# Two loads issued ahead of the last group's stores, and one sum moved from GpSimd to VectorE, in an AdaLN transformer layer

## The reference, cut to what matters

```python
x = data                                            # 2048 tokens x 1024
h = layernorm(x) * (1 + ca) + sa
x = x + ga * (h @ (weight * mask_by_32x32_blocks).T + bias)
h = layernorm(x) * (1 + cb) + sb                    # ca, sa, ... from silu(c) @ wmod
g = silu((h @ gate_w.T) * gate_s)                   # 2752 rows of gate_w, int32
u = (h @ up_w.T) * up_s
x = x + gb * (((g * u) @ down_w.T) * down_s)
```

## Time and profile before

| what | us |
|---|---|
| median of 3 runs | 1135.83 |
| the profiled execution | 1133.88 |
| its span | 1132.1 |
| TensorE busy | 1091.0 (96%) |
| VectorE busy | 787.1 (70%) |
| GpSimd busy | 412.1 (36%) |
| mean granted TensorE clock | 0.986 of full speed |

### The profile page before, as it was taken

How to read it: one execution, slowest core, us unless ns; L and a number is a source line. 1 busy time by engine, 2 the same in 40 slices (tenths; PEclk the granted TensorE clock), 3 DMA queues, 4 the chain that set the end, 5 groups by cost and what they waited for, 6 DMA issues and landing times. The chain is left out here.

```text
span 1132.1 us, 13073 instructions
## 1 busy us (share of the span) xinstructions
PE 1091.0 (96%) x4629; PEld 514.0 (45%) x4629; DVE 787.1 (70%) x966; ACT 423.3 (37%) x776; POOL 412.1 (36%) x365
## 2 busy tenths in 40 slices
PE   5996999999999999999999999999997999999998
PEld 3553554554444444434444444444443444444444
DVE  4789967767678898888897988879544343334434
ACT  0331236656555444445465555555432000000000
POOL 1223327546656363515675675755301000000000
PEclk9998989999999999999999999999998999999999
DMA  9993212426353565446676656665297666565430
GB/s 346 404 380 77 75 38 74 112 56 203 121 197 100 160 180 174 116 117 182 177 215 186 201 170 197 184 200 178 76 354 280 253 244 233 227 239 222 183 144 37
DMA packets 130000, 206.93 MB, mean 183 GB/s; under 512 B 20624, under 2 KB 99216, under 8 KB 127504
## 3 DMA queue, kind: packets, MB, share of 16 engines
q1 hardware_dynamic: 124640, 184.08, 49.4%
q0 software_dynamic: 5296, 22.02, 5.4%
HBM read 137.39 MB, written 68.68 MB: 182 GB/s over the span
## 5 line engine op out<-in xcount | busy, mean ns | idle before, releaser
L1295 PE MATMUL pA<-work 128*128 128x512 f16 x1680 | 378.6, 380 | 5.4 <-ACT work L1037 4.4
L1295 PEld LDWEIGHTS pA<-work 128*128 128x128 f16 x1680 | 164.1, 98 | 206.8 <-ACT work L1037 7.5
L1158 PE MATMUL pA<-work 128*128 128x512 f32 x512 | 227.2, 599 | 0.7 <-issue 0.7
L1295 PE MATMUL pB<-work 128*128 128x512 f16 x752 | 176.0, 379 | 1.8 <-DVE work L1726 1.8
L1748 DVE SCALAR_TENSOR_TENSOR work<-work 128x512 f16<-128x512 f16 x144 | 141.1, 1002 | 18.5 <-ACT work L1055 18.3
L1158 PEld LDWEIGHTS pA<-work 128*128 128x128 f32 x512 | 96.4, 193 | 113.4 <-issue 112.5
L1362 PE MATMUL pA<-work 128*128 128x512 f16 x600 | 136.1, 382 | 6.0 <-DMA work<-down_left_scratch 6.0
L912 ACT ACTIVATE work<-pB,small 128x128 f32<-128x128 f32 x256 | 92.7, 480 | 90.4 <-PE pB L1147 77.0
L1037 ACT ACTIVATE work<-pA 128x512 f32<-128x512 f32 x126 | 74.7, 593 | 114.6 <-PE pA L1295 108.6
L1295 PEld LDWEIGHTS pB<-work 128*128 128x128 f16 x752 | 73.4, 98 | 90.8 <-DVE work L1726 2.8
L1362 PE MATMUL pB<-work 128*128 128x512 f16 x480 | 107.5, 379 | 0.0
(11 more groups left out here) (170 smaller groups left out, 1159.4 us busy)
## 6 DMA issues: line engine op xcount, KB each, us to landing
work<-h_scratch SPq DMA_DIRECT2D x8, 4480.0 KB, 13.6
h_scratch<-work SPq DMA_DIRECT2D x60, 512.0 KB, 3.0
work<-in_L_wmod SPq DMA_DIRECT2D x10, 2048.0 KB, 18.0
work<-in_L_ffn_gate_w SPq DMA_DIRECT2D x84, 128.0 KB, 3.2
work<-in_L_ffn_up_w SPq DMA_DIRECT2D x84, 128.0 KB, 2.9
work<-down_scratch SPq DMA_DIRECT2D x7, 1280.0 KB, 15.6
work<-in_L_ffn_down_w SPq DMA_DIRECT2D x68, 128.0 KB, 2.8
work<-in_L_attn_data SPq DMA_DIRECT2D x16, 512.0 KB, 4.2
```

Source lines behind the costliest of these rows:

```text
L1158: last = pe.matmul(pA[:, 2 * par(t) + h, :], hT1[par(t)][:, c, :], wT[:, c, h * H:(h + 1) * H], start=(c == 0), stop=(c == KT - 1))
L1295: last = pe.matmul(ps, w[:, m, c], bc[b][:, mv_, s, c], start=begin, stop=(i == n - 1 and c == KT // 2 - 1 and s == 1), skip_group_check=True)
```

## The change

Two loads move in SP's queue: in pass NG - 1 wl and then WT1 are issued ahead of group 40's stores, and the wait for tail_ready in front of them goes (the stores of the tail one pass earlier have waited for the same count). For an odd chunk, S4 is no longer GpSimd's third operation: VectorE makes it, right after up[1] and ahead of the low part of S1, with a semaphore s4_ready of its own; s_ready now counts two for each odd group.

```diff
@@ SP, pass g
+                if g == NG - 1:
+                    sp.dma_start(wl..., wl_d...).then_inc(wl_loaded, 16)
+                    load_wd(WT1)
                 loads = [...]
                 ... the stores of group g - 1 ...
                 if g == NG - 1:
-                    sp.wait_ge(tail_ready, 4)
-                    load_wd(WT1)
-                    sp.dma_start(wl..., wl_d...).then_inc(wl_loaded, 16)
                     sp.wait_ge(p3_done, NG)
                     for m in (WT3, WT4, W22):
                         load_wd(m)
@@ GpSimd, odd_sums
-                pool.wait_ge(s_ready, n + 2)
-                pool.tensor_tensor(gate[1], up[0], keep[b][0], ALU.subtract).then_inc(s_ready, 1)
@@ ScalarE, hi_of
-                if m in (S1, S2, S4):
-                    act.wait_ge(s_ready, 3 * groups_before(g, "odd") + (S1, S2, S4).index(m) + 1)
+                if m in (S1, S2):
+                    act.wait_ge(s_ready, 2 * groups_before(g, "odd") + (S1, S2).index(m) + 1)
+                elif m == S4:
+                    act.wait_ge(s4_ready, groups_before(g, "odd") + 1)
@@ VectorE, wait_read
-                    dve.wait_ge(s_ready, 3 * groups_before(g - 1, "odd") + (3, 1)[half])
+                    dve.wait_ge((s4_ready, s_ready)[half], (1, 2)[half] * groups_before(g - 1, "odd") + 1)
@@ VectorE, pass g, behind hi_plus(up[1], ...)
                 if len(outs) > 2:
+                    dve.wait_ge(s_ready, 2 * groups_before(g - 1, "odd") + 2)
+                    dve.tensor_tensor(gate[1], up[0], keep[GROUPS[g - 1][1]][0], ALU.subtract).then_inc(s4_ready, 1)
+                if len(outs) > 2:
                     lo_of(g - 1, outs[2])
```

More of the change, by code:

```diff
@@ L349, in adaln_kernel @@
         s_ready = sem("s_ready")
+        s4_ready = sem("s4_ready")
         h2_hi = sem("h2_hi")
@@ L670, in _ @@
                         store_tail(sp, TAIL_BEFORE[g], half)
+                if g == NG - 1:
+                    sp.dma_start(wl.rearrange("p c k d -> p (c k d)"), wl_d.rearrange("p c k d -> p (c k d)")).then_inc(wl_loaded, 16)
+                    load_wd(WT1)
                 loads = [u for u in range(EARLY + 2, NUNIT) if g < NG and group_of[u - 2] == g]
@@ L697, in _ @@
                 if g == NG - 1:
-                    sp.wait_ge(tail_ready, 4)
-                    load_wd(WT1)
-                    sp.dma_start(wl.rearrange("p c k d -> p (c k d)"), wl_d.rearrange("p c k d -> p (c k d)")).then_inc(wl_loaded, 16)
                     sp.wait_ge(p3_done, NG)
@@ L838, in odd_sums @@
             def odd_sums(g):
-                b, n, before = GROUPS[g][1], 3 * groups_before(g, "odd"), partner(g)
+                b, n, before = GROUPS[g][1], 2 * groups_before(g, "odd"), partner(g)
                 pool.wait_ge(h2_lo, outs_until(before, S3))
```

## The result

Over twelve runs of each on the same chips, the changed kernel takes 1125.16 us (1122.59 to 1132.15) and the kernel before 1135.3 us (1132.66 to 1137.79): a ratio of 0.9916, 95% interval 0.9902 to 0.9930, or 9.5 us less (7.9 to 11.1; the two medians lie 10.1 apart). The forecast was 4.5 us less, 1131.3 (1127.3 to 1133.8).

What follows compares the result with a forecast made beforehand. The prediction took TensorE's waits as the bound. Removed 8.3 us (6.00 + 1.87 + 0.42), added stall 2.6 and clock 1.7, second stage -0.5: net -4.5, from 1135.83 to 1131.3 us, range 1127.3 to 1133.8.

Steps and rivals of the forecast that it cites:

- The loads, issued earlier: Down stage's start: wl and WT1 land near 855, removing a 6.00 us wait and 1.87 us of clock.
- the 0.42 us: Second stage's last product: its 0.42 us wait for VectorE would go, since up[1] is made sooner.
- What is late next: Pair 1's start: load_h2(1)'s small part lands at 892.4, TensorE is ready at 889.8, so it idles 2.6 us.
- The sum moved: Second stage: S4 on VectorE gives -0.5 us, bounds -1.5 and +1.6, besides the 0.42 us wait removed.
- the four places: Second stage, where TensorE's p7 needs the snapshot following gate[1]: each was to lose 0.25 us, 1.0 in all.
- kind (a): Odd groups whose low parts overlap L846: VectorE gains 0 to 0.1 us, up[1] comes sooner, two low parts take about 1.9.
- D: Rival: SP's queue for pair 1 gets no shorter, stall 7.6 us there; +0.7 us, 1136.5; chance 0.09.
- E: Rival: VectorE's subtraction lands on the path in all odd groups, 12 us; +8, 1143.8; chance 0.06.
- The 2.23 us stall: Second stage, TensorE behind VectorE's gate_b in an even group: claimed to stay at 2.23 us.
- the new stall and its clock: Pair 1's start: TensorE stalls 2.6 us, then loses 1.7 us to a lowered clock.
- B: Rival: the new stall at pair 1 costs no clock; -6.2 us, 1129.6; chance 0.23.
- C: Rival: pair 1's data comes sooner, stall 0.8 us or less; -8.0 us, 1127.8; chance 0.17.

Runs made afterwards that it cites:

- loads_only: Kernel before with only the two loads issued early, S4 still on GpSimd; 1128.05 us, ratio 0.9947.
- waits_loads: Kernel before with the two early loads and two redundant VectorE waits per odd group, last sum still on GpSimd; 1125.3 us, ratio 0.9913.
- gate_b_held: Changed kernel with VectorE's product of up[0] at gate_b made to wait for GpSimd's first sum of chunk 9; 1132.9 us, one run.
- small_first: Changed kernel with each pair's small load issued ahead of its big one; 1126.18 us, ratio 0.9914.
- after_again: Changed kernel, nothing altered, run and profiled a second time; 1125.51 us in one run.
- waits_after: Kernel before with two redundant VectorE waits only in the odd groups' passes behind group 13; 1137.68 us, one run.

## Why the prediction was off

**Right.** *The loads, issued earlier*: both waits and the 1.87 us of clock are gone, all 7.9 us; the 0.42 us, which the forecast credited to the sum, went with the sum, since loads_only keeps 0.41. wl and WT1 land at 848.0 and 851.9, 3 us sooner than said, because they begin 1.4 us sooner and move in the working time too: the window 841 to 850 now carries 394 GB/s where the earlier trace rows had 340. *What is late next*: the place, the transfer and the order were right; the issue of the small part was forecast 20.0 us after the down stage's start and came at 20.45, and TensorE was ready at 33.1 where 32.8 was said (0.17 us of this is the way of counting, 0.13 a gap between two products). *The sum moved*, taken proper: forecast -0.42 - 0.5 = -0.9 us, measured 507.42 - 508.35 = -0.9 against waits_loads. But its pieces differ, and that they add up is luck. The 1.54 us stall went and a 0.62 for VectorE came in its place at 408.27; the four places that were to lose 0.25 each, 1.0 in all, lost 0.16 at two (0.33 to 0.49) and nothing at two. GpSimd's L846 is gone and kind (a)'s low parts take 1.71 and 1.79 us for two, as said (1.9). Rivals D and E are refuted: the queue did get shorter, and the 20 subtractions (0.68 us each) cost nothing on the path. WT3 is issued 2.2 us after the down stage's start, WT1 was 1.7 after it.

**The step that failed:** "The 2.23 us stall comes from a chain (gate_b) in an even group and stays." It shrank by 1.23 us, and with it went the 1.7 us of clock behind it: 2.9 of the 6.0 us by which the traces differ from the forecast. The chain is as described, but it is fed by a collision 9 us earlier that 0.36 us in VectorE's stream decide. I asked which instructions the change touches, and not which neighbours were within a fraction of a microsecond of another order. The trace before had the sign: a product of 1.62 us begun 0.08 us behind a sum of GpSimd, where its like at 504.71 takes 0.75.

**The terms that were mis-sized:** the new stall and its clock, 2.6 + 1.7 = 4.3 us, measured 0.87 + 0 (0.87 to 1.85 in seven profiles of kernels without padding or a held product). The stall took 15.4 us for the landing; in the profiles with the early loads it is 13.4 to 15.7 and once 17.1, since the small load lands anywhere in that scatter, and 15.4 was one draw from its upper half. The eight pairs of the kernel before, which the forecast could have asked for, landed in 13.6 to 15.7 us, median 14.6 (after: 13.4 to 16.0, median 14.5). The median would have been the better choice, and gives a stall of 1.8. The clock followed from the stall: of the ten profiles in the table the eight with up to 1.85 us lost none, and those with 3.98 and 4.53 us lost 1.57 and 1.39. At 2.6 us itself nothing was run; at 2.2 us the traces hold both, lost in the kernel before and kept in gate_b_held. Of the rivals, B had the mechanism, a stall of 2.0 us or less without cost in clock: that holds in all seven. C, a stall of 0.8 or less, is nearly met in three of them (0.87 to 0.97) and not in the other four (1.44 to 1.85). Less the 2.9 us of the second stage, which neither had, B's time is 1126.7 us and C's 1124.9, beside the 1125.16 measured. The estimate for a pair's transfer that was set against the row, 13.0 us by the Trainium skill (DMA: Bandwidth & Descriptors, section Anatomy of one DMA — SWDGE (gpsimd) path), lies just below everything seen at pair 1 (13.3 us and more). That the 15.4 us came of other transfers in the queue, as the prediction has it, is not shown; small_first shows that the pair's own big load holds the small one back.

**The sums side by side.** Down stage -8.3 + 4.3 = -4.0 with the 0.42 us; measured -6.7 - 0.4 in the profile shown, -6.1 - 0.4 in after_again. Second stage -0.5; measured -3.4 without the 0.42, of which 2.9 are the stall at gate_b and its clock. In total -4.5 against -10.5 in the trace and -9.5 in the timed runs, whose scatter includes later landings than the profile's.

## What to carry to other kernels

Two loads issued earlier removed their own wait in full here; what such a move leaves is read from the next transfer in the same queue, with the median and the spread of its landings and not with the one row nearest in time. Before saying that a stall stays, look a few microseconds upstream for an operation of VectorE and one of GpSimd that begin within some tenths of a microsecond of each other: here a change over 60 us ahead in VectorE's stream turned their order. And run the edit's empty twin, here two waits that wait for nothing, before an effect is credited to what the edit does.

## What was not expected of the hardware

- Six redundant waits on VectorE, over 60 us ahead of the place, made the kernel's second stage 2.9 us shorter (511.30 to 508.40): 0.36 us directly, 0.87 by the order of two operations and 1.7 by the clock. Where a short instruction transfer of queue q14 lies goes with it.
- A stall of 2.2 us cost 1.7 us of clock in all profiles of the kernel before, loads_only and waits_after, and nothing in gate_b_held. The granted clock is full ahead of it in each. What makes the difference stays open. Longer stalls cost 1.39 to 2.83 us, with no order by their length: 5.43 us cost 2.83, and 6.60 us cost 1.45.
- The 192 KB load of pair 1, second in the queue behind 4480 KB, landed 13.4 to 17.1 us after its issue; issued first it landed in 2.3 and 3.2 us, and the 4480 KB then took 14.2 and 14.8 in place of 13.3 to 13.7.
